# Layer-1 expert weights kept in SBUF, and a slot's output product three slots behind its first products

## What is computed

```python
flat = _rmsnorm(x, ln2_w).reshape(-1, Cx)
probs = jax.nn.softmax(flat @ router_w.T, axis=-1)
tp, ti = jax.lax.top_k(probs, TOPK)
tp = tp / (jnp.sum(tp, axis=-1, keepdims=True) + 1e-09)
weights = jnp.sum(tp[..., None] * jax.nn.one_hot(ti, NE, dtype=flat.dtype), axis=1)
for e in range(NE):
    hh = jax.nn.silu(flat @ w1[e].T) * (flat @ w3[e].T)
    out = out + weights[:, e:e + 1] * (hh @ w2[e].T)
```

## Time and profile before

| | us |
|---|---|
| median of the runs (619.45 to 745.92) | 620.7 |
| the profiled execution, its own time | 617.0 |
| its span in the trace | 614.8 |
| PE matmul busy | 507.4 (83%) |
| PE weight loads busy | 283.2 (46%) |
| DVE busy | 433.6 (71%) |
| ACT busy | 319.9 (52%) |
| POOL busy | 272.5 (44%) |

### The profile page before, as it was taken

How to read it: one execution, slowest core, us unless ns; L and a number is a source line. 1 busy time by engine, 2 the same in 40 slices (tenths; PEclk the granted TensorE clock), 3 DMA queues, 4 the chain that set the end, 5 groups by cost and what they waited for, 6 DMA issues and landing times. The chain is left out here.

```text
span 614.8 us, 12091 instructions
## 1 busy us (share of the span) xinstructions
PE 507.4 (83%) x3865; PEld 283.2 (46%) x3865; DVE 433.6 (71%) x1076; ACT 319.9 (52%) x533; POOL 272.5 (44%) x310
## 2 busy tenths in 40 slices
PE   2999986699999799977766887998968768978881
PEld 1533334477777454534322323333412257766770
DVE  6998848978999935576793886998761068545454
ACT  0777986769999001110334544763744465535451
POOL 3000006133436402332183895996444527866542
PEclk9999996999999999997685989999979799989995
DMA  8999954000039340112034221003015145666665
GB/s 302 416 421 422 399 183 161 19 19 20 28 130 410 95 100 0 33 39 76 0 103 103 70 66 23 1 1 81 11 50 168 39 106 167 172 186 184 169 192 164
DMA packets 46086, 81.92 MB, mean 133 GB/s; under 512 B 8112, under 2 KB 37600, under 8 KB 41680
## 3 DMA queue, kind: packets, MB, share of 16 engines
q1 hardware_dynamic: 42304, 76.33, 38.1%
q0 software_dynamic: 2272, 4.69, 2.2%
q10 hardware_dynamic: 1456, 0.22, 0.2%
HBM read 61.72 MB, written 17.11 MB: 128 GB/s over the span
## 5 line engine op out<-in xcount | busy, mean ns | idle before, releaser
L1275 ACT ACTIVATE A<-ps 128x1024 f32<-128x1024 f32 (+3 forms) x80 | 68.6, 893 | 54.4 <-PE ps L1712 42.4
L2358 DVE TENSOR_REDUCE A<-ps 128x1 f32<-128x512 f32 (+3 forms) x160 | 86.1, 602 | 11.5 <-PE ps L1620 10.9
L969 POOL TENSOR_TENSOR G<-G,A 128x1024 f32<-128x1024 f32 (+3 forms) x40 | 73.9, 1890 | 16.8 <-ACT A L1275 16.7
L1369 PE MATMUL ps<-R,G 128*128 128x512 f32 x128 | 59.2, 605 | 1.1 <-DVE G L1920 0.8
L1620 PE MATMUL ps<-A 96*128 96x512 f16 (+3 forms) x160 | 53.5, 373 | 7.4 <-DVE A L2358 4.9
L1543 PE MATMUL ps<-A,G 128*128 128x512 f32 x128 | 59.2, 594 | 0.0
L1823 PE MATMUL ps<-A 128*128 128x128 f16 (+1 forms) x702 | 50.4, 226 | 5.4 <-issue 5.0
L1471 PE MATMUL ps<-R 128*128 128x128 f16 x768 | 48.3, 220 | 6.7 <-DVE x L2038 5.8
L1712 PE MATMUL ps<-A 97*128 97x512 f16 (+3 forms) x160 | 46.3, 375 | 8.1 <-ACT A L1275 8.1
L1471 PEld LDWEIGHTS ps<-R 128*128 128x128 f16 x768 | 45.4, 98 | 14.3 <-issue 6.6
L2020 DVE SCALAR_TENSOR_TENSOR R<-R 128x512 f16<-128x512 f32 x64 | 46.5, 750 | 7.0 <-ACT R L1130 6.8
(11 more groups left out here) (315 smaller groups left out, 948.8 us busy)
## 6 DMA issues: line engine op xcount, KB each, us to landing
A<-in_adj_t SPq DMA_DIRECT2D x16, 1024.0 KB, 17.6
A<-w_split SPq DMA_DIRECT2D x39, 341.0 KB
slots_in<-xn SPq DMA_DIRECT2D x1, 8320.0 KB, 22.4
R<-in_adj_in SPq DMA_DIRECT2D x7, 1024.0 KB, 5.7
xn<-in_adj_in SPq DMA_DIRECT2D x5, 1024.0 KB, 12.9
xT<-in_adj_in SPq DMA_DIRECT2D x4, 1024.0 KB, 12.6
A<-in_f_w SPq DMA_DIRECT2D x16, 170.5 KB
w_split<-A SPq DMA_DIRECT2D x8, 341.0 KB, 5.0
```

Source lines behind the costliest of these rows:

```text
L969: pool.tensor_tensor(total, total, probabilities(n, pair)[:, :, t0:CW], ALU.add).then_inc(s_sum, 1)
L1275: act.activation(probabilities(n, pair)[:, :, t0:CW], ps[:, 2 * pair:2 * pair + 2, t0:CW], ACT.Exp, scale=1.0 / (SQ * SQ * float(HD) ** 0. ...
L1369: last = pe.matmul(ps[:, c, :], G[:, j, :], fbuf[:, j % FB, CW * c:CW * c + CW], start=(j == 0), stop=(j == NT - 1))
L2358: dve.reduce_max(pm[:, h, t % TPC, b:b + 1], ps[:, bank, 0:width], AX_X).then_inc(s_rmf, 1)
```

## The change

The halves of `w1` and `w3` no longer go through HBM. `w13` is now two views in SBUF, of the high and the low halves, that hold all eight experts; `high_weights` and `low_weights` write there. `w_split`, `store_split` and `load_first` are gone, and with them 8 stores and 39 loads of 341 KB. Experts are prepared in the order `PREPARED`, at partly other steps. `hidden1` reads the expert's number into a register itself, ahead of its matmuls, and its weights' addresses hang on that register; `output1` uses the same register three turns later and no longer reads it. `output1` follows three slots behind `hidden1`, not two, with a fourth pair in `g16`; `copy_output` moves with it. SP loads the slots' rows in 12 batches with a semaphore each.

```diff
@@ places and order of the weights
-        v13s = A16[:, 12:16, 4 * CW:4 * CW + 2 * H1].rearrange("p (s n) w -> p s n w", s=2)
+        v13 = A[:, 14:16, 2 * CW:2 * CW + 2 * H1]
+        v2 = A[:, 6:12, 2 * CW - D:2 * CW].rearrange("p (s k) d -> p s k d", s=2)
-        w13 = [A16[:, j:j + 2, o:o + 2 * H1] for j, o in w13_at]
+        w13 = [A16[:, 6:6 + E1, o:o + 2 * H1] for o in (0, 4 * CW)]
+        PREPARED = (6, 7, 0, 1, 2, 3, 4, 5)
-        XB = 6
-        BATCHES = (1, 2, 3, 3, 4, 4, 1, 3, 4, 4, 4, 4, 2)
+        XB = 12
+        BATCHES = (1, 2, 3, 3, 4, 4, 1, 3, 4, 4, 5, 5)
+        g16 += [A16[:, 13, 7 * CW:7 * CW + 3 * P], g_last[:, :]]
-        PREPARE_AT = {(0, 1): 0, (0, 2): 1, (0, 3): 2, (1, 2): 3, (1, 5): 4, (2, 4): 5, (2, 8): 6, (3, 4): 7}
+        PREPARE_AT = {(0, 1): 0, (0, 2): 1, (1, 3): 2, (1, 5): 3, (2, 1): 4, (2, 4): 5, (2, 8): 6, (3, 4): 7}
-        LOW_AT = {(0, 1): 0, (0, 2): 1, (1, 0): 2, (1, 2): 3, (1, 5): 4}
+        LOW_AT = {(0, 1): 0, (0, 2): 1, (1, 4): 2, (1, 6): 3, (2, 2): 4}
@@ sync
+            def load_expert1(n):
+                s, e = n % 2, PREPARED[n]
+                if n >= 2:
+                    sp.wait_ge(s_wlo, n - 1)
...
-            def store_split(e):
-                sp.wait_ge(s_wlo, e + 1)
-                sp.dma_start(w_split[e, :, 0:W13].rearrange("p (n w) -> p n w", n=2), v13s[:, e % 2]).then_inc(s_wst[e % 2], 16)
-                if e + 2 < E1:
-                    load_expert1(e % 2, e + 2)
...
-            load_expert1(0, 0)
-            load_expert1(1, 1)
-            store_split(0)
+            load_expert1(0)
+            load_expert1(1)
+            load_expert1(2)
             stack(2, True)
-            store_split(1)
+            load_expert1(3)
             stack(2, False)
             stack_row_max(1)
-            store_split(2)
             stack(3, True)
             stack(3, False)
-            store_split(3)
-            store_split(4)
+            load_expert1(4)
+            load_expert1(5)
             stack_row_max(2)
+            load_expert1(6)
             stack_row_max(3)
-            for e in (5, 6, 7):
-                store_split(e)
...
-            def load_first(n):
-                g = 0 if n < FIRST else 1
-                i = n - IDS[g][0]
-                if i == 0:
-                    sp.wait_ge(s_route, EXPERTS_KNOWN[g])
-                if n >= WB:
-                    sp.wait_ge(s_h3, n - WB + 1)
-                e = sp.value_load(expert_i[g][0:1, i:i + 1], min_val=0, max_val=E1 - 1)
-                sp.dma_start(w13[n % WB], w_split[bass.ds(e, 1), :, :].rearrange("a p (n w) -> (a p) n w", n=2)
-                             ).then_inc(s_w13l[n % WB], 16)
+            load_expert1(7)
...
-            for n in range(WB):
-                load_first(n)
             sp.wait_ge(s_negT, NC)
             sp.wait_ge(s_od, NC - 1)
-            for b in range(4):
+            for b in range(len(BATCHES)):
                 load_slot_rows(b)
-            b = 4
-            for n in range(WB, SLOTS):
-                load_first(n)
-                if b < len(BATCHES) and n - WB + ROWS_AHEAD >= ENDS[b] - BATCHES[b]:
-                    load_slot_rows(b)
-                    b += 1
@@ scalar
-                if k >= 3:
-                    copy_output(k - 3)
+                if k >= 4:
+                    copy_output(k - 4)
@@ tensor
             def hidden1(n):
-                pe.wait_ge(s_w13l[n % WB], AGAIN + 16 * (n // WB + 1))
+                g = 0 if n < FIRST else 1
+                i = n - IDS[g][0]
+                if n == 0:
+                    pe.wait_ge(s_wlo, E1)
+                if i == 0:
+                    pe.wait_ge(s_route, EXPERTS_KNOWN[g])
+                expert[n] = pe.value_load(expert_i[g][0:1, i:i + 1], min_val=0, max_val=E1 - 1)
                 pe.wait_ge(s_sxl, n + 1)
...
-                            last = pe.matmul(ps[0:w, bank + n % 2, P * k:P * k + P], w13[n % WB][:, part, o:o + w], a,
+                            last = pe.matmul(ps[0:w, bank + n % 2, P * k:P * k + P], w13[part][:, bass.ds(expert[n], 1), o:o + w].rearrange("p a w -> p (a w)"), a,
                                              start=i == 0, stop=i == 2, skip_group_check=True)
...
             def output1(n):
...
-                e = pe.value_load(expert_i[g][0:1, i:i + 1], min_val=0, max_val=E1 - 1)
+                e = expert.pop(n)
                 pe.wait_ge(s_glo, n + 1)
...
-                hi, lo = g16[2 * (n % 3)], g16[2 * (n % 3) + 1]
+                hi, lo = g16[2 * (n % 4)], g16[2 * (n % 4) + 1]
...
-                if k >= 2:
-                    output1(k - 2)
+                if k >= 3:
+                    output1(k - 3)
```

More of the change, by code:

```diff
@@ L459, in program @@
         AGAIN = 16
-        s_xr, s_w13l = [*s_A[0:4], s_A[10], s_A[15]], s_A[4:4 + WB]
-        assert len(s_xr) == XB and WB <= 6
+        s_xr = [*s_A[0:11], s_A[15]]
+        assert len(s_xr) == XB
         s_squares, SQUARES = s_first, 16 * 3
@@ L995, in _ @@
                     clear_sums(c)
-                if (c, turn) == (1, 0):
-                    low_weights(LOW_AT[(1, 0)])
                 add_to_sums(n)
@@ L1247, in router_exp, with high_weights @@
                 act.activation(lg1[:, 2, w], lg1[:, 6, w], ACT.Exp).then_inc(s_re, 1)
-            def high_weights(e):
-                act.wait_ge(s_ld1[e % 2], AGAIN + 64 * (e // 2 + 1))
-                if e >= 2:
-                    act.wait_ge(s_wst[e % 2], AGAIN + 16 * (e // 2))
-                flat2 = v2[:, e % 2].rearrange("p k d -> p (k d)")
-                act.activation(v13s[:, e % 2, 0].rearrange("p (m h) -> p m h", m=2), v13[:, e % 2], ACT.Copy, scale=factor[:, 3:4])
-                act.activation(w2[:, e, 0:3 * D], flat2, ACT.Copy, scale=SW)
-                act.activation(v13[:, e % 2], v13[:, e % 2], ACT.Copy, scale=factor[:, 3:4])
-                act.activation(flat2, flat2, ACT.Copy, scale=SW).then_inc(s_whi, 1)
+            def high_weights(n):
+                s, e = n % 2, PREPARED[n]
+                act.wait_ge(s_ld1[s], AGAIN + 64 * (n // 2 + 1))
+                if n == 2:
+                    act.wait_ge(s_klo, NC)
+                act.activation(w13[0][:, e, :], v13[:, s], ACT.Copy, scale=factor[:, 3:4])
+                act.activation(by_k(w2[:, e, 0:3 * D]), v2[:, s], ACT.Copy, scale=SW)
+                act.activation(v13[:, s], v13[:, s], ACT.Copy, scale=factor[:, 3:4])
+                act.activation(v2[:, s], v2[:, s], ACT.Copy, scale=SW).then_inc(s_whi, 1)
             def slot_high(n):
@@ L1313, in high_hidden @@
                 act.wait_ge(s_hh, n + 1)
-                if n >= 3:
-                    act.wait_ge(s_y1, n - 2)
-                act.activation(g16[2 * (n % 3)], g32[n % 2], ACT.Copy).then_inc(s_ghi, 1)
+                if n >= 4:
+                    act.wait_ge(s_y1, n - 3)
+                act.activation(g16[2 * (n % 4)], g32[n % 2], ACT.Copy).then_inc(s_ghi, 1)
             def copy_output(n):
@@ L1337, in _ @@
             high_hidden(SLOTS - 1)
-            for n in range(SLOTS - 3, SLOTS):
+            for n in range(SLOTS - 4, SLOTS):
                 copy_output(n)
@@ L1795, in rows_there @@
             def rows_there(b):
-                return AGAIN + 16 * sum(BATCHES[b % XB:b + 1:XB])
+                return AGAIN + 16 * BATCHES[b]
             def slot_transpose(n):
-                pe.wait_ge(s_xr[batch_of[n] % XB], rows_there(batch_of[n]))
+                pe.wait_ge(s_xr[batch_of[n]], rows_there(batch_of[n]))
                 if n == 0:
@@ L1807, in slot_transpose @@
                 pe.transpose(ps[:, x_bank(n), 0:P], slot_rows(n)[:, 0:D], ident[:, :]).then_inc(s_sT, 1)
+            expert = {}
             def hidden1(n):
[L1811 removed]
+                g = 0 if n < FIRST else 1
[5 more added lines that the diff above has]
+                expert[n] = pe.value_load(expert_i[g][0:1, i:i + 1], min_val=0, max_val=E1 - 1)
                 pe.wait_ge(s_sxl, n + 1)
@@ L1854, in _ @@
             slot_transpose(0)
-            for k in range(SLOTS + 2):
+            for k in range(SLOTS + 3):
                 if k + 1 < SLOTS:
```

47 lines of the change are left out of this document (17 added, 30 removed).

## The result

| | before | after |
|---|---|---|
| median of the runs | 620.7 us (3 runs) | 647.21 us (4 runs) |
| profiled execution: span | 614.8 us | 645.3 us |
| first products of slot 0 / 3 / 38 | 495.82 / 503.12 / 597.05 | 499.99 / 509.74 / 628.12 |
| mean turn, slots 3 to 38 | 2.68 us | 3.38 us |

The changed kernel is slower: ratio 1.043, 95% interval 1.0382 to 1.0479. A fourth run of before took 745.92 us, in a slower state that single executions show, and is left out of the median and the ratio. The forecast was 645 us.

A forecast was written before the change was run, and what follows sets the result against it. PE was taken to set the slot loop's pace. On 617.0 us: loop +21.6, slots 0 to 2 +2, small units +0.4, end +0.5, attention 0, together +24.5, 641.5; plus 3.7 to the median's scale, 645 us; range 628 to 664.

The forecast's parts named there:

- A turn: Slot loop on PE: read, first products with address instructions, output and transpose sum to 3.28 us, taken as 3.3.
- Loop 3 to 38: Slots 3 to 38: 35 turns of 3.3 us, 115.5 against 93.9 us, +21.6.
- Both costs exposed: PE's sequencer: the read (0.86 us, 39 times) and the address instructions (36 ns each) are not hidden behind queued matmuls.
- The gain that was there to win: Slot loop before: 23 us of waits and half clock, of which the change is meant to remove up to 23 us.
- unexplained stalls: PE stalls without a known cause, left out of the forecast turn; up to 5 us in the forecast's own range.
- Rival (B): Slot loop: read and address instructions both hide, turn 2.05 us, -22, about 599 us; chance 4%.
- Slots 0 to 2: First turns: three reads and 36 address instructions, less an output product and about 1 us hidden under waits: +2 us.
- End: Behind slot 38's first products: its own products take 0.4 us longer, two outputs fit under the chain: +0.5 us.
- Attention: The 8 preparations move among the chunks; 2.4 us more subtractions fit in 3.2 us free: 0, 1 us either way.
- The sum: All terms together +24.5 us on the profiled execution, 641.5 us; 645 us on the scale of the runs' median.
- Rival (C): Slot loop: thin matmuls bring half clock; with the read exposed on top, turn 3.96 us, about 670 us; chance 8%.
- Rival (A): `hidden1`: its address instructions hide and cost nothing, turn 2.9 us, time 626 to 630 us; chance 8%.

The follow-up runs named there:

- the moved read: Kernel after with the next slot's number read right behind `hidden1`'s matmuls, address instructions kept: 648.26 us beside after's 650.01, ratio to before 1.0365, turn 3.377 us.

## Why the prediction was right, and where it was off

**A turn.** Forecast 0.07 + 0.86 up to the first product, 1.36 + 0.2 for `hidden1`, 0.79 for the output: 3.28, taken as 3.3. In the trace 0.94, 1.69, 0.75: 3.38. The first and the last pieces hold. The middle one was mis-sized by 0.13: an address instruction adds (1.57 - 1.06) / 11 = 46 ns on average to the run of loads, and not the 36 ns that I took from before's output. That this equals the length of its record is chance: its steps on the sequencer are some 125 ns long, and one or two loads of 56 ns pass in each. Loop 3 to 38: +24.5 measured, +21.6 forecast.

**Both costs exposed.** Right, and the moved read shows it. The sum adds them, and while the sequencer sets the turn they do add (1.89 + 12 x 0.125 = 3.39). But it holds only down to the turn that the waits set. Taking the 12 away saved 0.79 us of the mean and not 1.49; moving the read as well gave nothing more, and having no read and no address instruction at all 0.12 us more (2.467). What I wrote as evidence for an exposed read, that `output1` leaves no queue, was wrong as a general statement: in the kernel with fixed addresses in `hidden1` the sequencer's lead outlasts the output's six. The output loads of the earlier trace rows, from which I took the 36 ns, stand behind before's read, which had used the lead up.

**The gain that was there to win.** I wrote that up to 23 us of waits in before's turns were what the change was meant to remove. Part of the 23 is half clock (0.50 between 549.21 and 552.31, the turn of the earlier trace rows). The waits do disappear in after, where a turn of 3.38 us covers VectorE's 1.65, ScalarE's 1.50 and GpSimd's 1.69 us, and the granted clock is 1.00. The up to 5 us of unexplained stalls in the range are the 5.0 us put down to "issue" in the earlier trace rows; in after 20.3 us are, all in front of `hidden1`, the read's place. But with residency and without its costs the turn is 2.58 us against 2.68, and the time is the same. Rival (B)'s 599 us, a turn of 2.05, was out of reach for another reason than the one I gave: even with no address instruction and no read the mean turn was 2.47 us.

**Slots 0 to 2.** +2.45 us (7.30 to 9.75), forecast +2. The agreement is not evidence for the three reads and 36 address instructions: the granted clock there was 1.00 in before's profile and 0.66 in after's, and the kernel before without the range test, whose sequencer has less to do than before's, took 9.62 us at 0.52. The four profiles of kernels with after's instructions on the sequencer lie between 8.09 and 9.76 us. **End.** From slot 38's first products to the span's end 17.75 us before, 17.2 after: -0.6, forecast +0.5. The last outputs run without a gap right behind `hidden1`.

**Attention.** The step that failed: "I count 0, with 1 us either way". The loop starts 4.2 us later in after's profile. Profiles on the slower chips spread: with before's attention the loop starts at 495.8, 498.2 and 501.5, with after's at 499.3, 500.0, 500.0, 502.1, 503.1 and 504.9. So part of the 4.2 can be the profile's own spread. By ScalarE's end copies 1.0 of it was there at the end of the third chunk (424.92, 425.89), 2.1 came in the fourth (62.64, 64.71 us) and 1.1 behind it, where PE's granted clock was 1.00 in before and 0.50 in after for the last 6 us ahead of the loop. On the chip where the clock was full through the fourth chunk, its length (end copies of third and fourth chunk) compares cleanly, first the kernel before with the extra read:

```profile
427.50:477.10 49.60, 48.55 (x420) 18.09 (x418) 27.82 (x111) 34.10 (x48) 25.86 (x31) 1.00 0.34 99
```

and the kernel after without the range test:

```profile
426.80:477.70 50.90, 48.55 (x420) 18.03 (x418) 29.68 (x111) 34.08 (x48) 27.94 (x32) 1.00 0.12 37
```

The chunk is 1.3 us longer (1.7 in the two kernels with reads of four), with the same PE time and 1.9 us more of VectorE and 2.1 us more of GpSimd in it. GpSimd's pair (1.49 + 0.92 us) that the change puts into the third chunk ends its last sums 2.9 us later (420.55 to 423.46), and 3.2 us was the slack that I had read from the earlier trace rows; it was read for the matmuls on the sums, and not for what GpSimd and VectorE do next. What they do next is the instruction of VectorE that ends only with GpSimd's subtractions, and ScalarE's wait for it: 0.8 to 1.3 us, gone when the pair is put behind the chunk. What the sum had at nothing was this wait. How much of it reaches the slot loop was not shown, and adding such a pair to the kernel before was not tried; the rest of the delay stays open.

**The sum.** Forecast +24.5 us on the profiled execution; its span grew by 30.5, of which the loop's 24.5 are the mechanism, 2.45 slots 0 to 2 with the clock in them, 4.2 the start, -0.6 the end. The medians differ by 26.5 us, so this pair of profiles overstates the difference by some 4 us. That the forecast of the time, 645 against 647, came so close is in part luck: the loop came out 2.9 us above its term, and on the medians all the others together 0.9 below theirs, although single ones were off by up to 4 us in the profile. Rival (C)'s thin matmuls at half clock did not occur: the clock was 1.00 from slot 3 to slot 38. That matmuls so thin would bring the half clock of the earlier trace rows was my estimate, and no run showed it. Rival (A), address instructions that hide, is refuted by the 1.57 us run.

## What to carry to other kernels

In these kernels operands whose addresses come from a register took instructions on TensorE's own sequencer, 12 for the 18 matmuls of `hidden1` and 6 for the 9 of `output1`: 46 ns each in the record, some 125 ns of the sequencer's time in `hidden1`. So before turning a load with a dynamic address into a matmul with one, add up what the sequencer has to do in a turn (here 12 more address instructions, 1.5 us, on top of 1.9) and compare it with the turn that the matmuls (1.6 us) and the waits (2.5 to 2.7 us) set. Below that, in the kernel before, the second read added 0.12 us to the mean turn, and leaving out the range test made no difference that could be measured (ratio 0.9981). Above it, in after, leaving out the range test took 0.27 us off every turn. And before paying for the removal of a transfer, take the transfer away with wrong data at a fixed address: here the kernel with fixed addresses and the read behind, a run of that kind, showed nothing to be won.

## What the runs showed of the hardware

- In `hidden1` of after the starts of two address instructions stand some 125 ns apart in most places, whether one or two matmuls lie between them; 12 of them make 1.5 us, where 18 matmuls at fixed addresses take 1.0 (56 ns each). So, worked out from these, an address used once adds some 70 ns to the run of loads and one shared by two matmuls hardly more than 10.
- A read of one number into a TensorE register took 0.30 us as an instruction (median of 39 in after); with the range test and all, 0.68 to 0.76 us of after's turn. An extra one added 0.5 us to a turn without a wait in the kernel before, but 0.12 us to its mean, because waits disappeared.
- A read of four numbers in one instruction took 0.53 us in the median and up to 1.11 us, that is 0.13 to 0.28 us a number against 0.30 for one at a time. In the turn shown it held back the next first product by 1.15 us (536.66 to 538.07, less 0.26).
- In the kernel whose slots all share one register, the address instructions of `hidden1` were made once for all of them (12, not 468). So that kernel measures more than the read it takes out.
- Every mean turn of a kernel with after's 18 address instructions and one full read in a turn was between 3.377 and 3.382 us, in four profiles, with a granted clock of 0.56 to 0.76 in slots 0 to 2 and 1.00 from slot 3 to slot 38; mean turns that are set by waits ranged from 2.58 to 2.69 (before, before with the output three behind or without the range test, and the two with fixed addresses and one read).
- An instruction of VectorE on two operands in SBUF (128x32), whose kind took 0.19 us right behind it, took 2.7 to 5.6 us while GpSimd subtracted the weights' halves, and ended some 0.05 us after GpSimd's last subtraction, in all fourteen profiles.
